# Group normalisation in two batches and weight peaks in three groups, in the front of a recurrent kernel

## The chip, the cores and the metric

The kernel runs on one core of one Trainium2 chip. The metric is the device time of one execution in microseconds (us); the figure for a kernel is the median over its runs. PE is TensorE, PEld its weight loads, DVE VectorE, ACT ScalarE, POOL GpSimd, SP the engine that issues the DMAs.

## The reference, cut to what matters

```python
def _gn(v, G=32, eps=1e-05):                 # v is 8 x 128 x 32 x 32
    g = v.reshape(B_, G, C_ // G, H_, W_)
    m, s = mean and variance of g over (channels of a group, H, W)
    return ((g - m) / sqrt(s + eps)).reshape(v.shape)

def step(h, xr):                             # one row (or column) of 8 images
    gi, gh = xi @ wih.T, h @ whh.T           # 3 gates of 128 channels each
    r, z = sigmoid(ir + hr), sigmoid(iz + hz)
    n = tanh(i_n + r * h_n)
    ctx = (1 - z) * n + z * h
    h_new = tanh(conv1d(ctx, cw, cb))        # 3 taps along the row
    return h_new, ctx

# 32 steps in each of three directions: down, up, and right to left; then
out = x + einsum('bchw,oc->bohw', concat(ctx_d, ctx_u, ctx_r), w_comb) + b_comb
```

## The kernel before

The 128 channels lie on the 128 partitions. Three recurrences (k = 0, 1, 2) of 32 steps run interleaved. Every float32 product is made of three float16 ones: an operand is scaled and split into a high part (`HI`, its float16 rounding) and a low part (`LO`, what is left), and HI·HI, LO·HI and HI·LO are added in PSUM. That holds for weights (`w_parts`), for the normalised images (`x_rows`), for the contexts and for the hidden state.

Each engine has its own instruction stream, written out by hand in the order in which it is to run; an instruction waits on semaphores, and everything behind it in that stream waits with it. SP issues two weight loads (k = 0, 1), eight image loads (512 KB each), then the weights of k = 2 and of the combination.

The front, up to the first real product, does two things.

1. **Weights.** A set of weights (7 of them: the gates and the convolution of each k, and the combination) is scaled by a power of two that comes from its largest row sum. ACT sums magnitudes (`magnitude_sums`, L418), PE turns the sums into rows (`turn_sums`, L811), DVE takes the maximum (`sets_peak`, L642 and L644), PE spreads it over the partitions (`spread_peaks`, L817), DVE makes the scales (`weight_scales`, L653 to L659). Sets 0 to 3 go first, sets 4 to 6 later. Then each of ten units of three weight blocks is split: ACT makes the high part (`weights_hi`, L439), and the low part is made by POOL for four units (`in 0`, `rec 0`, `conv 0`, `in 1`, L388 and L393) and by DVE for six (`weights_lo`, L634).
2. **Images.** DVE takes the mean and variance of six images per channel (`image_stats`, L584 and L589, in the order 0, 2, 3, 5, 6, 7), ACT those of images 1 and 4 (`image_moments`). Then one chain for all eight images: PE averages the means over the groups (L834), DVE makes the deviations (`spread`, L596 to L601), PE averages those (L838), DVE adds epsilon (`variance`, L606), POOL takes the power -1/2 (L398), DVE makes the shift (`shift`, L612). Then both engines normalise the first and last four rows (`edges`, 128x256) of their images (DVE 0 to 4, ACT 5 to 7), and later the last four columns (`strip`, 128x96) and the `core` (128x672). From the normalised rows ACT makes the high part of each piece (`x_hi`, L453) and DVE the low part (`x_lo`, L626).

Between these PE runs products whose result nobody reads (`warm`, L823, 128x512 each): 12 (`FRONT_WARM`) before it waits for the image statistics, 4 (`CHAIN_WARM`) after each of three steps of the chain, and 7 (`LAST_WARM`) after it has waited for the shift (`x_factor`). The first real product (L849, `input_products(0, 0)`) waits for the first `x_hi`.

After that, `opening` (one for each engine) issues the first steps of the three recurrences with the remaining strips, pieces and weight units between them, and `blocks` the steady loop. At the end PE multiplies the contexts with the combination's weights, DVE adds the residual and SP stores.

In the steady part of the code a block needs the split rows, the weights' parts of its direction, and the hidden state of the step before.

Of the kernel before, what the change touches and what calls it, by code (L numbers as in the profile page):

```python
# [99 lines left out]
CORE_ON_ACT = {(1, 1): (5,), (1, 2): (6,), (2, 0): (7,)}  # L100
CORE_ON_DVE = {(1, 1): (0,), (1, 2): (1, 2), (2, 0): (3, 4)}


def build(nc, x_d, w_d, bias_d, out_d):
# [4 lines left out]
    with ExitStack() as ctx:  # L109
# [33 lines left out]
        peak = [sb(f"peak_{n}", [SETS, 1], f32) for n in range(2)]  # L143
        peak_diag = [sb(f"peak_diag_{n}", [SETS, SETS], f32) for n in range(2)]
# [38 lines left out]
        peak_bank = [conv_bank[0], n_bank[2]]  # L183
        avg_bank, var_bank = conv_bank[1], rz_bank[0]
# [176 lines left out]
        def _(pool):  # L361
# [23 lines left out]
            pool.wait_ge(scale_done, 1)  # L385
            for unit in range(len(POOL_UNITS)):
                n, lo, hi = unit_blocks(unit)
                nc.gpsimd.tensor_tensor(out=w_scaled32[:, unit, :], in0=merged(w32[:, lo:hi, :]),  # L388
# [8 lines left out]
            pool.wait_ge(var_eps, 1)  # L397
            nc.gpsimd.tensor_tensor(out=x_scale[:], in0=gvar[:], in1=minus_half[:], op=ALU.pow) \  # L398
                .then_inc(pow_done, 1)

        @block.scalar
        def _(act):
# [33 lines left out]
            def weights_hi(unit):  # L436
                n, lo, hi = unit_blocks(unit)
                act.wait_ge(scale_done, 1 if n < SET_GROUPS[0][1] else 2)
                nc.scalar.activation(w_parts[:, HI, lo:hi, :], w32[:, lo:hi, :], ACT.Copy,  # L439
                                     scale=w_scale[:, n:n + 1]).then_inc(w_hi_done, 1)  # L440

            def normalise(b, cells):

                act.wait_ge(x_factor, 1)
# [83 lines left out]
            def opening():  # L528
# [5 lines left out]
                for b in ACT_NORMED[0:2]:  # L534
                    normalise(b, strip)
# [3 lines left out]
                normalise(ACT_NORMED[2], strip)  # L539
# [29 lines left out]
        def _(dve):  # L569
# [23 lines left out]
            def spread():  # L593

                dve.wait_ge(mean_avg, 1)
                chain(nc.vector.tensor_tensor(out=dev[:], in0=meanvar[:, :, 0], in1=avg_bank[:, 0:B],  # L596
                                              op=ALU.subtract))
                chain(nc.vector.tensor_tensor(out=dev[:], in0=dev[:], in1=dev[:], op=ALU.mult))
                nc.vector.tensor_tensor(out=dev[:], in0=dev[:], in1=meanvar[:, :, 1],
                                        op=ALU.add).then_inc(spread_done, 1)  # L600
                nc.vector.tensor_copy(gmean[:], avg_bank[:, 0:B])  # L601

            def variance():

                dve.wait_ge(var_avg, 1)
                nc.vector.tensor_scalar(gvar[:], var_bank[:, 0:B], EPS, ACT_SCALE ** -2, ALU.add,  # L606
                                        ALU.mult).then_inc(var_eps, 1)

            def shift():

                dve.wait_ge(pow_done, 1)
                nc.vector.scalar_tensor_tensor(x_shift[:], gmean[:], -1.0, x_scale[:],  # L612
# [49 lines left out]
            dve_normed = [b for b in range(B) if b not in ACT_NORMED]  # L662
# [401 lines left out]
```

## Time and profile before

| | |
|---|---|
| time, median of 3 runs | 346.21 us (346.2 to 346.48) |
| the profiled execution | 346.73 us, its span 345.0 us |
| outside the span | 1.73 us |
| PE busy | 321.6 us (93% of the span) |
| DVE, ACT, POOL busy | 294.0, 252.6, 11.0 us |

The span runs from the first to the last instruction that the profiler recorded. Times within a run are given from its start. "Idle before" in a row is the time for which the engine did nothing ahead of that instruction, and the arrow names what ended it. Successive instructions of DVE and ACT overlap by 0.08 to 0.1 us in the records when the second doesn't wait for the first; matmuls overlap by more, so for PE the distance of two starts is what an instruction takes.

### The profile page before, as it was taken

How to read it: one execution, taken by the hardware profiler on the slowest of the kernel's cores; microseconds unless marked ns; L12 is line 12 of the kernel's file. 1: busy time of each engine (PE TensorE's matmuls, PEld its weight loads, DVE VectorE, ACT ScalarE, POOL GpSimd, SP SyncE). 2: the span in 40 equal slices, each digit the busy share in tenths (PEclk: the TensorE clock that was granted, in tenths of full speed). 3: DMA queues.
4: the chain of work that ended last, by engine and by line, in shares of the span. 5: the costliest groups of instructions: out<-in, count | busy, mean ns of one | idle time of the engine just before them, and what ended most of it. 6: DMA issues, size and time to landing. Idle time of an engine off the chain costs nothing.

```text
span 345.0 us, 7730 instructions
## 1 busy us (share of the span) xinstructions
PE 321.6 (93%) x2725; PEld 261.2 (76%) x2725; DVE 294.0 (85%) x781; ACT 252.6 (73%) x587; POOL 11.0 (3%) x24
## 2 busy tenths in 40 slices
PE   0589689999999999999999999999999999999995
PEld 0237568888888888888888888888888888874442
DVE  0878999999999999999989989888888888896342
ACT  5879988888888878788777777777777777767600
POOL 2540000000000000000000000000000000000000
PEclk9999999999999999999999999999999999999999
DMA  7900000000000000000000000000000000000555
GB/s 296 409 10 4 0 2 0 2 1 3 2 0 2 3 0 3 2 0 3 0 0 0 0 0 0 0 0 0 0 0 0 0 0 0 0 2 24 171 151 143
DMA packets 11251, 10.61 MB, mean 31 GB/s; under 512 B 2528, under 2 KB 9824, under 8 KB 11232
## 3 DMA queue, kind: packets, MB, share of 16 engines
q1 hardware_dynamic: 11232, 10.36, 8.9%
q8 instruction: 12, 0.20, 0.2%
q14 instruction: 7, 0.06, 0.1%
HBM read 6.16 MB, written 4.19 MB: 30 GB/s over the span
## 4 chain that ended last, share of the span: by engine, by line
PE 83%; DVE 6%; ACT 6%; DMA 2%; issue 1%; POOL 1%; POOLq 0%; SPq 0%; ACTq 0%; DVEq 0%
PE rz_bank L849 22%; PE conv_bank L849 17%; PE rz_bank L852 11%; PE n_bank L849 11%; PE conv_bank L852 8%; PE n_bank L852 5%; DMA x<-x_dram 2%; PE rz_bank L958 2%; PE n_bank L960 2%; PE n_bank L958 2%; PE rz_bank L960 2%; PE n_bank L962 2%; PE rz_bank L962 2%; ACT w_parts L439 1%; ACT ctx_store L445 1%
## 5 line engine op out<-in xcount | busy, mean ns | idle before, releaser
L849 PE MATMUL conv_bank<-ctx_store,w_parts 128*128 (+1 forms) x558 | 106.9, 273 | 4.7 <-DVE ctx_store L711 2.0
L849 PE MATMUL rz_bank<-x_rows,w_parts 128*128 128x256 f16 (+1 forms) x384 | 78.6, 273 | 0.4 <-ACT x_rows L453 0.4
L849 PE MATMUL rz_bank<-h_parts,w_parts 128*128 128x256 f16 x372 | 76.1, 273 | 0.8 <-DVE w_parts L634 0.8
L488 ACT ACTIVATE nval<-npre 128x256 f32<-128x256 f32 x93 | 38.7, 416 | 52.0 <-DVE npre L718 52.0
L476 ACT ACTIVATE rz<-rz_bank,descale 128x512 f32<-128x512 f32 x96 | 65.9, 686 | 9.2 <-PE rz_bank L849 1.4
L849 PEld LDWEIGHTS conv_bank<-ctx_store,w_parts 128*128 128x128 f16 x558 | 54.0, 97 | 18.6 <-DVE ctx_store L711 3.0
L852 PE MATMUL conv_bank<-ctx_store,w_parts 128*128 (+1 forms) x279 | 66.0, 273 | 0.0
L706 DVE SCALAR_TENSOR_TENSOR npre<-n_bank,descale,rz 128x256 f32<-128x256 f32 x93 | 45.0, 484 | 15.6 <-ACT rz L476 14.4
L852 PE MATMUL rz_bank<-x_rows,w_parts 128*128 128x256 f16 (+1 forms) x192 | 52.2, 273 | 0.0
L493 ACT ACTIVATE hval<-conv_bank,biases,descale 128x256 f32<-128x256 f32 x93 | 51.4, 553 | 0.0
L849 PE MATMUL n_bank<-x_rows,w_parts 128*128 128x256 f16 (+1 forms) x192 | 47.1, 273 | 0.0
L849 PE MATMUL n_bank<-h_parts,w_parts 128*128 128x256 f16 x186 | 45.7, 273 | 0.0
L852 PE MATMUL rz_bank<-h_parts,w_parts 128*128 128x256 f16 x186 | 45.7, 273 | 0.0
L718 DVE SCALAR_TENSOR_TENSOR npre<-n_bank,descale,npre 128x256 f32<-128x256 f32 x93 | 44.4, 477 | 0.0
L499 ACT ACTIVATE ctx_store<-context 128x272 f16<-128x272 f32 (+1 forms) x96 | 40.8, 425 | 2.1 <-DVE context L699 1.4
L699 DVE TENSOR_TENSOR context<-rz,nval 128x256 f32<-128x256 f32 x93 | 39.5, 425 | 3.2
L711 DVE SCALAR_TENSOR_TENSOR ctx_store<-context,ctx_store 128x272 f16<-128x272 f32 (+1 forms) x96 | 41.5, 432 | 0.5 <-ACT ctx_store L499 0.5
L849 PEld LDWEIGHTS rz_bank<-x_rows,w_parts 128*128 128x128 f16 x384 | 37.5, 98 | 5.3 <-issue 0.9
L691 DVE SCALAR_TENSOR_TENSOR nval<-rz,nval 128x256 f32<-128x256 f32 x96 | 40.0, 417 | 0.9 <-ACT nval L488 0.8
L849 PEld LDWEIGHTS rz_bank<-h_parts,w_parts 128*128 128x128 f16 x372 | 36.2, 98 | 5.6 <-DVE w_parts L634 1.1
L729 DVE TENSOR_TENSOR rz<-rz,hval 128x256 f32<-128x256 f32 x93 | 38.8, 417 | 0.0
L723 DVE SCALAR_TENSOR_TENSOR h_parts<-hval,h_parts 128x256 f16<-128x256 f32 x93 | 38.5, 414 | 0.3 <-ACT h_parts L504 0.3
(90 smaller groups left out, 408.9 us busy)
## 6 DMA issues: line engine op xcount, KB each, us to landing
x<-x_dram SPq DMA_DIRECT2D x8, 512.0 KB, 8.8
out_dram<-x_rows SPq DMA_DIRECT2D x7, 512.0 KB, 3.3
ctx_store<-weights_dram SPq DMA_DIRECT2D x3, 576.0 KB, 4.9
out_dram<-x_rows SPq DMA_DIRECT2D x2, 256.0 KB, 2.6
ctx_store<-weights_dram SPq DMA_DIRECT2D x1, 192.0 KB, 12.1
biases<-biases_dram SPq DMA_DIRECT2D x1, 2.0 KB, 11.7
```

The costliest lines, as they stand in the source:

```text
L476: nc.scalar.activation(rz[k][:].rearrange("p g c -> p (g c)"), rz_bank[k][:], ACT.Sigmoid, scale=gate_scale(k)).then_inc(sig_done[k], 1)
L488: nc.scalar.activation(nval[k][:], npre[k][:], ACT.Tanh).then_inc(n_done[k], 1)
L493: nc.scalar.activation(hval[k][:], conv_bank[k % 2][:, 0:COLS], ACT.Tanh, bias=biases[:, k:k + 1], scale=conv_scale(k)).then_inc(h_done[k], 1)
L499: nc.scalar.activation(context_lines(k, s, HI), context[k][:].rearrange("p l b -> p (l b)"), ACT.Copy, scale=ACT_SCALE).then_inc(ctx_hi_do ...
L691: nc.vector.scalar_tensor_tensor(nval[k][:], z, 1.0, nval[k][:], ALU.subtract, ALU.mult).then_inc(zn_done[k], 1)
L699: nc.vector.tensor_tensor(out=context[k][:, 1:1 + LINE, :], in0=lines(zh), in1=lines(nval[k][:]), op=ALU.subtract).then_inc(ctx_done[k], 1)
L706: nc.vector.scalar_tensor_tensor(npre[k][:], n_bank[k][:, COLS:2 * COLS], gate_scale(k), rz[k][:, 0, :], ALU.mult, ALU.mult).then_inc(rh_d ...
L711: nc.vector.scalar_tensor_tensor(context_lines(k, s, LO), context[k][:].rearrange("p l b -> p (l b)"), ACT_SCALE, context_lines(k, s, HI), ...
L718: nc.vector.scalar_tensor_tensor(npre[k][:], n_bank[k][:, 0:COLS], gate_scale(k), npre[k][:], ALU.mult, ALU.add).then_inc(npre_done[k], 1)
L729: nc.vector.tensor_tensor(out=rz[k][:, 0, :], in0=rz[k][:, 1, :], in1=hval[k][:], op=ALU.mult)
L849: last = nc.tensor.matmul(out, w_block(HI, k, n), parts(hi_or_lo), start=start, stop=stop and hi_or_lo == LO, skip_group_check=True)
L852: last = nc.tensor.matmul(out, w_block(LO, k, n), parts(HI), start=False, stop=False, skip_group_check=True)
```

## The change

The images are normalised in two batches, 0 to 3 and 4 to 7: the whole chain (average, `spread`, average, `variance`, power, `shift`) is issued once for each, on four columns instead of eight, into banks of its own. DVE now normalises images 0, 1, 4, 5, 6 and ACT 2, 3, 7. The two images of each engine that belong to the first batch get both edges and strip normalised in the front. The weight sets form three groups, (0, 1), (2, 3) and (4, 5, 6), and the first group's peak and scale stand ahead of all image statistics on DVE, the second's behind image 0. POOL makes the low part of five units (`conv 1` is added) and the low part of `rec 1` moves on DVE from the opening into the front. `FRONT_WARM` goes from 12 to 10, and those products now stand behind PE's second average of the first batch.

```diff
-ACT_NORMED = (5, 6, 7)
-SET_GROUPS = ((0, 4), (4, SETS))
+BATCHES = ((0, 4), (4, B))
+ACT_NORMED = (2, 3, 7)
+DVE_NORMED = (0, 1, 4, 5, 6)
+ACT_STAGES, DVE_STAGES = (0, 5, 6, 9), (0, 7, 10, 15)
+SET_GROUPS = ((0, 2), (2, 4), (4, SETS))
-FRONT_WARM, CHAIN_WARM, LAST_WARM = 12, 4, 7
+FRONT_WARM, CHAIN_WARM, LAST_WARM = 10, 4, 7
-POOL_UNITS = ("in 0", "rec 0", "conv 0", "in 1")
-DVE_UNITS = ("conv 1", "rec 1", "in 2", "conv 2", "rec 2", "comb")
+POOL_UNITS = ("in 0", "rec 0", "conv 0", "in 1", "conv 1")
+DVE_UNITS = ("rec 1", "in 2", "conv 2", "rec 2", "comb")
...
# gpsimd: the power, now after the five units and once for each batch
+            def inverse_deviation(batch):
+                ims = slice(*BATCHES[batch])
+                pool.wait_ge(var_eps, batch + 1)
+                nc.gpsimd.tensor_tensor(out=x_scale[:, ims], in0=gvar[:, ims], in1=minus_half[:, ims],
+                                        op=ALU.pow).then_inc(pow_done, 1)
...
# scalar: the wait of a weight unit, the wait of a piece, and the order
-                act.wait_ge(scale_done, 1 if n < SET_GROUPS[0][1] else 2)
+                act.wait_ge(scale_done, 1 + sum(n >= end for _, end in SET_GROUPS))
...
-                act.wait_ge(x_normed, normed * (B - len(ACT_NORMED)))
-                act.wait_ge(x_normed_act, normed * len(ACT_NORMED))
+                act.wait_ge(x_normed, DVE_STAGES[normed])
+                act.wait_ge(x_normed_act, ACT_STAGES[normed])
...
+            for unit in range(3):
+                weights_hi(unit)
             image_moments(ACT_IMAGES[0])
-            for unit in range(2):
-                weights_hi(unit)
+            weights_hi(UNITS.index("in 1"))
             image_moments(ACT_IMAGES[1])
-            for unit in range(2, UNITS.index("in 2")):
-                weights_hi(unit)
+            for unit in ("conv 1", "rec 1"):
+                weights_hi(UNITS.index(unit))
             for k in (2, COMB):
                 magnitude_sums(k)
-            for b in ACT_NORMED:
-                normalise(b, edges)
+            for cells in (edges, strip):
+                for b in ACT_NORMED[0:2]:
+                    normalise(b, cells)
+            normalise(ACT_NORMED[2], edges)
...
# vector: the order of the front
-            image_stats(0)
             sets_peak(0)
             weight_scales(0)
-            for b in (2, 3, 5, 6, 7):
+            image_stats(0)
+            sets_peak(1)
+            weight_scales(1)
+            for b in (2, 3, 5):
                 image_stats(b)
-            spread()
-            weights_lo(UNITS.index("conv 1"))
-            variance()
-            sets_peak(1)
-            shift()
-            for b in dve_normed:
+            spread(0)
+            image_stats(6)
+            variance(0)
+            image_stats(7)
+            spread(1)
+            shift(0)
+            normalise(DVE_NORMED[0], edges)
+            variance(1)
+            normalise(DVE_NORMED[1], edges)
+            for b in DVE_NORMED[0:2]:
+                normalise(b, strip)
+            weights_lo(UNITS.index("rec 1"))
+            sets_peak(2)
+            shift(1)
+            for b in DVE_NORMED[2:]:
                 normalise(b, edges)
-            normalise(dve_normed[0], strip)
+            normalise(DVE_NORMED[2], strip)
...
# vector: the opening
                 blend(0, 0)
-                for b in dve_normed[1:3]:
-                    normalise(b, strip)
+                normalise(DVE_NORMED[3], strip)
                 context_lo(0, 0)
                 blend(1, 0)
-                for b in dve_normed[3:]:
-                    normalise(b, strip)
+                normalise(DVE_NORMED[4], strip)
                 context_lo(1, 0)
-                weights_lo(UNITS.index("rec 1"))
                 hidden_lo(0, 0)
...
# tensor: the front
-            turn_sums(0)
-            spread_peaks(0)
+            def average(batch, dve_images, act_images):
+                ims = slice(*BATCHES[batch])
+                pe.wait_ge(aggr_done, dve_images)
+                pe.wait_ge(act_stats, 2 * act_images)
+                nc.tensor.matmul(avg_bank[batch][:, ims], group_avg[:], meanvar[:, ims, 0],
+                                 start=True, stop=True).then_inc(mean_avg, 1)
+
+            def average_variance(batch):
+                ims = slice(*BATCHES[batch])
+                pe.wait_ge(spread_done, batch + 1)
+                nc.tensor.matmul(var_bank[batch][:, ims], group_avg[:], dev[:, ims],
+                                 start=True, stop=True).then_inc(var_avg, 1)
+
+            for n in range(2):
+                turn_sums(n)
+                spread_peaks(n)
+            average(0, 3, 1)
             pe.wait_ge(w_hi_done, 2)
+            average_variance(0)
             warm(FRONT_WARM)
-            pe.wait_ge(aggr_done, B - len(ACT_IMAGES))
-            pe.wait_ge(act_stats, 2 * len(ACT_IMAGES))
-            nc.tensor.matmul(avg_bank[:, 0:B], group_avg[:], meanvar[:, :, 0],
-                             start=True, stop=True).then_inc(mean_avg, 1)
+            average(1, B - len(ACT_IMAGES), len(ACT_IMAGES))
             warm(CHAIN_WARM)
-            pe.wait_ge(spread_done, 1)
-            nc.tensor.matmul(var_bank[:, 0:B], group_avg[:], dev[:],
-                             start=True, stop=True).then_inc(var_avg, 1)
+            average_variance(1)
             warm(CHAIN_WARM)
-            turn_sums(1)
+            turn_sums(2)
             warm(CHAIN_WARM)
-            spread_peaks(1)
-            pe.wait_ge(x_factor, 1)
+            spread_peaks(2)
+            pe.wait_ge(x_factor, 2)
             warm(LAST_WARM)
```

The rest of the diff gives `spread`, `variance` and `shift` a batch argument and the columns `ims` of that batch, and moves ACT's strip of its third image a few places up in its opening, with the other two strips gone from there.

## Rows read from the trace of the kernel before

**Rows 1.** Windows: length, busy us and count by engine, clock, DMA share, GB/s.
```profile
24.80:52.00 27.20, 21.73 (x186) 17.18 (x186) 25.11 (x69) 24.19 (x55) 0.00 (x0) 1.00 0.01 2
52.00:306.00 254.00, 253.90 (x2324) 222.97 (x2325) 237.03 (x642) 197.04 (x466) 0.00 (x0) 1.00 0.00 1
```

**Rows 2.** Timeline of DVE, image statistics: start us, length us, what.
```profile
8.19 1.29 DVE L584 BATCH_NORM_STATS2 stats<-x 128x6 f32<-128x512 f32 x2 [8.19 <-DMA x<-x_dram]
...
9.63 0.23 DVE L642 TENSOR_REDUCE peak<-conv_bank 4x1 f32<-4x128 f32 x1
...
11.48 1.28 DVE L584 BATCH_NORM_STATS2 stats<-x 128x6 f32<-128x512 f32 x2
...
16.00 1.23 DVE L584 BATCH_NORM_STATS2 stats<-x 128x6 f32<-128x512 f32 x2
...
17.39 1.23 DVE L584 BATCH_NORM_STATS2 stats<-x 128x6 f32<-128x512 f32 x2
```

**Rows 3.** Timeline of DVE, the chain behind the statistics.
```profile
19.35 0.16 DVE L596 TENSOR_TENSOR dev<-meanvar,conv_bank 128x8 f32<-128x8 f32 x1 [0.48 <-PE conv_bank L834]
...
19.91 0.61 DVE L634 SCALAR_TENSOR_TENSOR w_parts<-ctx_store,w_scale,w_parts 128x384 f16<-128x384 f32 x1
20.43 0.16 DVE L606 TENSOR_SCALAR gvar<-rz_bank 128x8 f32<-128x8 f32 x1
21.59 0.28 DVE L642 TENSOR_REDUCE peak<-n_bank 3x1 f32<-3x128 f32 x1 [0.99 <-PE n_bank L811]
21.90 0.22 DVE L644 TENSOR_SCALAR peak_diag<-unit_diag,peak 3x3 f32<-3x3 f32 x1
...
22.44 1.95 DVE L616 TENSOR_SCALAR ctx_store<-x,gmean,x_scale 128x256 f32<-128x256 f32 x6
```

**Rows 4.** Timeline of PE in the front.
```profile
7.74 0.58 PE L811 MATMUL conv_bank<-unit_diag,abs_sum 128*4 128x128 f32 x2 [7.74 <-ACT x_rows L418]
...
13.49 4.47 PE L823 MATMUL rz_bank<-w_parts 128*128 128x512 f16 x12 [2.74 <-ACT w_parts L439]
18.93 0.39 PE L834 MATMUL conv_bank<-meanvar,group_avg 128*128 128x8 f32 x2 [0.97 <-DVE meanvar L589]
19.17 1.02 PE L823 MATMUL rz_bank<-w_parts 128*128 128x512 f16 x4
...
22.45 0.38 PE L817 MATMUL n_bank<-peak_diag,ones 3*128 3x3 f32 x2
22.76 1.69 PE L823 MATMUL rz_bank<-w_parts 128*128 128x512 f16 x7
24.88 0.27 PE L849 MATMUL rz_bank<-x_rows,w_parts 128*128 128x256 f16 x1 [0.43 <-ACT x_rows L453]
```

**Rows 5.** The chain that ended last: start us, length us, what.
```profile
24.30 0.44 ACT x_rows L453
```

**Rows 6.** Timeline of ACT, weight sums and high parts.
```profile
6.01 0.19 ACT L418 ACTIVATION_READ_ACCUMULATOR x_rows<-ctx_store 128x1 f32 x1
...
12.33 1.10 ACT L439 ACTIVATE w_parts<-ctx_store,w_scale 128x384 f16<-128x384 f32 x2
```

**Rows 7.** Timeline of PE's weight loads during the twelve unread products.
```profile
13.89 0.15 PEld L823 LDWEIGHTS rz_bank<-w_parts 128*128 128x128 f16 x1 [0.28 <-issue]
...
16.88 0.58 PEld L823 LDWEIGHTS rz_bank<-w_parts 128*128 128x128 f16 x3 [0.28 <-issue]
```

**Rows 8.** Groups by form, 18.9 to 26.2 us, a strip: busy us, mean ns.
```profile
L616 DVE TENSOR_SCALAR ctx_store<-x,gmean,x_scale 128x96 f32<-128x96 f32 x1 | 0.3, 331 | 0.0
```

**Rows 9.** Timeline of POOL, the power.
```profile
20.67 1.65 POOL L398 TENSOR_TENSOR x_scale<-gvar,minus_half 128x8 f32<-128x8 f32 x1 [1.03 <-DVE gvar L606]
```

**Rows 10.** Timeline of PE in the opening.
```profile
32.33 0.38 PE L849 MATMUL rz_bank<-h_parts,w_parts 128*128 128x256 f16 x2
...
36.50 0.28 PE L849 MATMUL conv_bank<-ctx_store,w_parts 128*128 128x256 f16 x1 [1.50 <-DVE w_parts L634]
```

**Rows 11.** Timeline of ACT in the opening, the gates of step 1.
```profile
32.91 0.67 ACT L476 ACTIVATE rz<-rz_bank,descale 128x512 f32<-128x512 f32 x1
```

More of the change, by code:

```diff
@@ L142, in build @@
         ones = sb("ones", [SETS, C], f32)
-        peak = [sb(f"peak_{n}", [SETS, 1], f32) for n in range(2)]
-        peak_diag = [sb(f"peak_diag_{n}", [SETS, SETS], f32) for n in range(2)]
+        peak = [sb(f"peak_{n}", [SETS, 1], f32) for n in range(len(SET_GROUPS))]
+        peak_diag = [sb(f"peak_diag_{n}", [SETS, SETS], f32) for n in range(len(SET_GROUPS))]
         image_sum = sb("image_sum", [C, len(ACT_IMAGES)], f32)
@@ L182, in build @@
         y_bank = [rz_bank[0], n_bank[0], rz_bank[1], n_bank[1]]
-        peak_bank = [conv_bank[0], n_bank[2]]
-        avg_bank, var_bank = conv_bank[1], rz_bank[0]
+        peak_bank = [conv_bank[0], n_bank[1], n_bank[2]]
+        avg_bank, var_bank = [conv_bank[1], n_bank[0]], [rz_bank[0], rz_bank[1]]
         w_loaded = [sem(f"w_loaded_{k}") for k in range(DIRS + 1)]
@@ L383, in _ @@
                 nc.gpsimd.memset(context[k][:, 0:PAD:PAD - 1, :], 0.0).then_inc(sides_zero, 1)
-            pool.wait_ge(scale_done, 1)
+            def inverse_deviation(batch):
[3 more added lines that the diff above has]
+                                        op=ALU.pow).then_inc(pow_done, 1)
             for unit in range(len(POOL_UNITS)):
                 n, lo, hi = unit_blocks(unit)
+                pool.wait_ge(scale_done, 1 + sum(n >= end for _, end in SET_GROUPS))
                 nc.gpsimd.tensor_tensor(out=w_scaled32[:, unit, :], in0=merged(w32[:, lo:hi, :]),
@@ L395, in _ @@
                     .then_inc(w_lo_pool, 1)
-            pool.wait_ge(var_eps, 1)
-            nc.gpsimd.tensor_tensor(out=x_scale[:], in0=gvar[:], in1=minus_half[:], op=ALU.pow) \
-                .then_inc(pow_done, 1)
+            for batch in range(len(BATCHES)):
+                inverse_deviation(batch)
         @block.scalar
@@ L442, in normalise @@
             def normalise(b, cells):
-                act.wait_ge(x_factor, 1)
+                act.wait_ge(x_factor, 1 if b < BATCHES[0][1] else 2)
                 nc.scalar.activation(cells(x_norm[:, b // 2, :, :, b % 2]), cells(x32[:, b, :, :]), ACT.Identity,
@@ L533, in opening @@
                 new_value(1, 0)
-                for b in ACT_NORMED[0:2]:
-                    normalise(b, strip)
+                normalise(ACT_NORMED[2], strip)
                 context_hi(1, 0)
@@ L538, in opening @@
                 hidden_hi(0, 0)
-                normalise(ACT_NORMED[2], strip)
                 x_hi(FIRST_COLS[0], 2)
@@ L590, in image_stats, with spread, variance, shift @@
                     .then_inc(aggr_done, 1)
-            def spread():
-                dve.wait_ge(mean_avg, 1)
-                chain(nc.vector.tensor_tensor(out=dev[:], in0=meanvar[:, :, 0], in1=avg_bank[:, 0:B],
+            def spread(batch):
+                ims = slice(*BATCHES[batch])
+                dve.wait_ge(mean_avg, batch + 1)
+                chain(nc.vector.tensor_tensor(out=dev[:, ims], in0=meanvar[:, ims, 0], in1=avg_bank[batch][:, ims],
                                               op=ALU.subtract))
-                chain(nc.vector.tensor_tensor(out=dev[:], in0=dev[:], in1=dev[:], op=ALU.mult))
-                nc.vector.tensor_tensor(out=dev[:], in0=dev[:], in1=meanvar[:, :, 1],
+                chain(nc.vector.tensor_tensor(out=dev[:, ims], in0=dev[:, ims], in1=dev[:, ims], op=ALU.mult))
+                nc.vector.tensor_tensor(out=dev[:, ims], in0=dev[:, ims], in1=meanvar[:, ims, 1],
                                         op=ALU.add).then_inc(spread_done, 1)
[L601 to L606, printed above, removed]
+                nc.vector.tensor_copy(gmean[:, ims], avg_bank[batch][:, ims])
+            def variance(batch):
+                ims = slice(*BATCHES[batch])
+                dve.wait_ge(var_avg, batch + 1)
+                nc.vector.tensor_scalar(gvar[:, ims], var_bank[batch][:, ims], EPS, ACT_SCALE ** -2, ALU.add,
                                         ALU.mult).then_inc(var_eps, 1)
-            def shift():
-                dve.wait_ge(pow_done, 1)
-                nc.vector.scalar_tensor_tensor(x_shift[:], gmean[:], -1.0, x_scale[:],
+            def shift(batch):
+                ims = slice(*BATCHES[batch])
+                dve.wait_ge(pow_done, batch + 1)
+                nc.vector.scalar_tensor_tensor(x_shift[:, ims], gmean[:, ims], -1.0, x_scale[:, ims],
                                                ALU.mult, ALU.mult).then_inc(x_factor, 1)
```

10 lines of the change are left out of this document (5 added, 5 removed).

## The prediction

> **What bounds the kernel now.** I read the windows first. From 52 to 306 us PE is busy for 253.90 of 254.00 us, and nothing that the change touches runs there. So the time is the moment at which PE gets into that stretch, plus a fixed rest. From 24.80 to 52.00 us PE still stands idle for 27.20 - 21.73 = 5.5 us [rows 1]; ahead of that is the front, where PE does no real work at all. The change can move the end in two ways only: by the start of the first real product, now 24.88 us [rows 4], and by the idle time of the opening.
>
> Next I read the chain of waits backwards from that product. It waits for the first x_hi (24.30 us, 0.44 us long) [rows 5], that for the normalised edges, those for the shift, the power, the variance, the averages, and the averages for image 7's statistics on DVE [rows 2, 3]. Once the second image has begun at 11.48, DVE goes from image to image in steps of about 1.4 us (16.00, 17.39) [rows 2]. Behind image 7 it waits: 0.48 us for the mean, 0.99 us before the second peak [rows 3]. Those holes are what two batches could fill.
>
> **The change, step by step on DVE.** The first group's weight sums end at 6.01 + 0.19 = 6.20 [rows 6]. Passing them to PE costs some 0.1, PE's turning product 0.58 [rows 4], and from the reduction to the next image DVE needs 11.48 - 9.63 = 1.85 (peak, PE's spreading, four small operations) [rows 2]. 6.20 + 0.1 + 0.58 + 1.85 = 8.8 (8.77, with a handover of 0.04). Image 0 could start at 8.19, so it starts 0.6 late: the first group is not quite done in the idle time. Image 0 takes 9.63 - 8.19 = 1.44, the second group 1.85 again, images 2, 3 and 5 1.44 each (their data are there: before, all this was over at 16.00). 8.8 + 1.44 + 1.85 + 3 x 1.44 = 16.41, where DVE stood at 16.00.
>
> spread(0) costs 19.91 - 19.35 = 0.56 [rows 3]: 16.97. Image 6 takes 17.39 - 16.00 = 1.39 [rows 2], variance(0) 0.08 (its 0.16 less the overlap), image 7's statistics and their handover to PE 18.93 - 17.39 = 1.54 [rows 2, 4]. So the second average *could* go at 16.97 + 1.39 + 0.08 + 1.54 = 19.98, 1.05 behind the 18.93 of before.
>
> **The step that decides: PE.** PE's stream is now average(0), average_variance(0), ten unread products, average(1). average_variance(0) waits for spread(0), whose third operation ends at 16.98 (0.57 from its first); with 0.06 of handover PE takes it at about 17.05. Before, the twelve products began at 13.49, as soon as two weight units were there [rows 4]. Behind them in PE's stream stands everything else: average(1), for which DVE's spread(1) waits, and behind that on DVE shift(0), every edge and strip; for those wait ACT's normalise and x_hi, and for these PE's real products.
>
> What ten products cost is in the trace. The weight loads of the first products follow each other at (16.88 - 13.89) / 7 = 0.427 us; 512 columns in 0.427 us is the lower level of 1.2 GHz. From about 16.9 on the last three starts fit in 0.7 us, 0.22 each, the 2.4 GHz level [rows 7, 4]. PE had done almost nothing before 13.49, and it will have done as little before 17.05. The float32 average costs 0.24 from start to next start at the high level (18.93 to 19.17) [rows 4], at half the clock 0.48; it would end at about 17.5. If the clock rises after as long a run of products as before (3.4 us), eight of ten run at 0.427 and two at 0.22: 3.86 us, and average(1) goes at 21.36 instead of 19.98. **Held for 1.38 us.** All ten at the low level give 4.27 and 21.77; a rise one and a half microseconds earlier gives about 20.6. The profile's clock column (1.00 throughout) doesn't show these two levels; the durations do.
>
> The Trainium skill, page "TensorE: Matmul & The Clock Gate", Part 1, says that the array starts at the lower clock after idling and that the point at which it rises varies from run to run. The trace agrees in the first part (0.427, then 0.22); the second no row of one execution can show, and it is what the rival of the late clock stands on. The same page, Part 2, says that matmuls stay in program order and only weight loads are pulled ahead: by that the average can't overtake the ten products. The sum above takes the order from the code.
>
> **The rest of the chain.** From the average to the variance it was 20.43 - 18.93 = 1.50 [rows 3, 4]: 21.36 + 1.50 = 22.86. Then DVE: variance 0.08; the edges of image 1, (1.95 - 0.33) / 5 = 0.32 [rows 3, 8]; two strips of 0.33 less 0.09 overlap, 0.48 [rows 8]; rec 1's low part 20.43 - 19.91 = 0.52 [rows 3]; the reduction 0.31 and the diagonal 0.13 [rows 3]. shift(1) at 24.70. The power is 1.65 for eight columns [rows 9]; for four I can say only that it is no more, and no less than nothing. At 1.65 it runs from 23.10 to 24.75 and costs 0.08 at most; below 1.6, nothing. I take nothing: DVE's other work covers it. Were that work gone, it would cost up to 1.65. Three edges follow: 0.09 + 3 x 0.32, ending at 25.84 with the last one's tail. x_hi starts at 25.87, ends at 26.30, and PE could take it at 26.44.
>
> But LAST_WARM comes in the way. The third group's diagonal ends at 24.79, PE spreads it at 24.85, the seven products start 0.31 later (22.76 - 22.45) [rows 4] and take 7 x 0.215 = 1.51: PE is free at 26.67. Before, 22.76 + 1.51 = 24.27 was well ahead of 24.88. First real product at **26.67, 1.79 later** than 24.88.
>
> **Edits costed at nothing.** ACT has its three high parts done 1.6 us after 8.9 (1.10 for two) [rows 6], and both its images by about 16.8, ahead of PE's average(1). The low part of conv 1 on POOL ends near 18.3, ahead of the first power and far ahead of its use. ACT's four operations on images 2 and 3 fit between shift(0) at 22.3 and the end of DVE's shift(1) at 24.87. No DMA is moved.
>
> **The opening.** DVE loses rec 1's low part (0.52) and two strips (0.48), ACT two strips. Little of it was on the path: DVE's removed work stood ahead of operations that waited for ACT anyhow. ACT's gates of step 1 start at 32.91, behind ACT's own queue, while their products were done at 32.33 + 0.38 = 32.71 [rows 10, 11]; with a handover of 0.12 they can go at 32.83. 0.08 us is won, and it carries through to the largest hole, 1.50 us before 36.50 [rows 10], which hangs on DVE's queue behind those gates. Bounds: 0 and, if all of DVE's 1.0 us came off that hole, 1.0. I take 0.08, since the chain from PE to ACT to DVE stays as long.
>
> **Sum.** 1.79 - 0.08 = 1.71 us. On the profiled execution, 346.73 + 1.7 = 348.4 (span 346.7); the median lies 0.52 below that execution: 346.21 + 1.71 = **347.9 us**, 0.5% slower. What a measurement of this kernel can tell from no change is about 0.2%, 0.69 us.
>
> **The rivals.**
> - *No hold on PE.* The clock rises early enough, or the ten products are over by 19.98. Then everything is 1.38 less: 346.21 + 0.33 = 346.54. For it: in the trace the average had 0.97 us to spare [rows 4]. Against: ten products after 17.5 need to take 2.5 us, and at the lower level alone they take 4.27. Chance 0.19.
> - *Faster: the opening's holes shrink.* If the full 1.0 us of freed DVE work comes off the hole before 36.50 and PE is not held, 1.79 - 1.38 - 1.0 = -0.6; with the seven last products not binding either (0.2), -0.8, 345.4. It decides only when PE's hold is below 0.1 us. Against: the waits for ACT in that stretch. Chance 0.13.
> - *Late clock.* If the rise comes only after some 6 us, average(1) goes at 21.77 and the four products behind it take 1.7 instead of 0.9, the next ones too: variance(1) 1.2 to 1.5 later than in the sum, in all 3 to 3.5: 349.5. Chance 0.12.
> - The forecast, PE held by 0.6 to 1.8 us: 347.0 to 348.7, chance 0.56.
>
> **Range.** 346.0 to 349.2 holds the forecast, the rival without hold and the milder half of the late clock; it leaves out 0.12 below and 0.06 above. Slower by over 0.2%: 0.56 + 0.12 = 0.68. Faster: 0.12. Within: 0.20.
>
> **What the new profile would show.** Image 0 on DVE at 8.8; spread(0) at 16.4; the ten unread products on PE from 17.5 to past 21, without a gap before average(1), and DVE idle for 1.4 us or more before spread(1), released by PE; the first real product at 26.7, straight behind the seven. I am wrong if DVE doesn't wait before spread(1), if the first real product starts below 25.6, or if the hole before the convolution of k = 2, step 0 is shorter than 1.2 us.

## The result and the profile after

The changed kernel takes 350.92 us (median of 4 runs, 350.38 to 351.17) against 346.35 for the kernel before: ratio 1.0135, 95% interval 1.0123 to 1.0147. The forecast was 347.9, the range ended at 349.2. The direction was right, the loss is 4.57 us instead of 1.7. The profiled execution is the fastest of the four, 350.38 us (span 348.7).

Timeline of DVE in the changed kernel, front, to be compared with [rows 2, 3].

```profile
8.83 1.28 DVE L593 BATCH_NORM_STATS2 stats<-x 128x6 f32<-128x512 f32 x2
...
10.27 0.22 DVE L654 TENSOR_REDUCE peak<-n_bank 2x1 f32<-2x128 f32 x1
10.53 0.31 DVE L656 TENSOR_SCALAR peak_diag<-unit_diag,peak 2x2 f32<-2x2 f32 x1
11.52 0.16 DVE L665 TENSOR_SCALAR pow<-n_bank 128x2 int32<-128x2 int32 x1 [0.68 <-PE n_bank L836]
11.71 0.91 DVE L668 TENSOR_SCALAR descale<-pow 128x2 f32<-128x2 f32 x1
12.65 0.17 DVE L670 RECIPROCAL w_scale<-pow 128x2 f32<-128x2 f32 x1
12.85 0.55 DVE L671 TENSOR_SCALAR w_scale<-w_scale 128x2 f32<-128x2 f32 x1
13.32 1.27 DVE L593 BATCH_NORM_STATS2 stats<-x 128x6 f32<-128x512 f32 x2
...
17.53 0.10 DVE L606 TENSOR_TENSOR dev<-meanvar,conv_bank 128x4 f32<-128x4 f32 x1
17.68 0.82 DVE L608 TENSOR_TENSOR dev<-dev 128x4 f32<-128x4 f32 x1
...
18.69 1.27 DVE L593 BATCH_NORM_STATS2 stats<-x 128x6 f32<-128x512 f32 x2
...
21.46 0.21 DVE L598 BATCH_NORM_AGGREGATE meanvar<-stats 128x2 f32<-128x12 f32 x1
23.80 0.16 DVE L606 TENSOR_TENSOR dev<-meanvar,n_bank 128x4 f32<-128x4 f32 x1 [2.13 <-PE n_bank L851]
...
25.71 0.61 DVE L646 SCALAR_TENSOR_TENSOR w_parts<-ctx_store,w_scale,w_parts 128x384 f16<-128x384 f32 x1
```

Image 0 starts at 8.83, as worked out. Then four operations on two or four columns, which cost 0.16 to 0.22 us in every other place of this trace, take 0.31, 0.91, 0.55 and 0.82. The second weight group, from its reduction at 10.27 to the next image, costs 13.32 - 10.27 = 3.05 us instead of 1.85, spread(0) 18.69 - 17.53 = 1.16 instead of 0.56. And DVE waits 2.13 us for PE ahead of spread(1).

Timeline of POOL, the same kernel.

```profile
9.91 0.91 POOL L402 TENSOR_TENSOR w_parts<-ctx_store,w_parts 128x384 f16<-128x384 f32 x1
10.78 0.83 POOL L397 TENSOR_TENSOR ctx_store<-ctx_store,w_scale 128x384 f32<-128x384 f32 x1
11.69 0.91 POOL L402 TENSOR_TENSOR w_parts<-ctx_store,w_parts 128x384 f16<-128x384 f32 x1
12.55 0.83 POOL L397 TENSOR_TENSOR ctx_store<-ctx_store,w_scale 128x384 f32<-128x384 f32 x1
...
17.57 0.91 POOL L402 TENSOR_TENSOR w_parts<-ctx_store,w_parts 128x384 f16<-128x384 f32 x1 [0.65 <-ACT w_parts L447]
...
25.07 1.11 POOL L391 TENSOR_TENSOR x_scale<-gvar,minus_half 128x4 f32<-128x4 f32 x1 [3.74 <-DVE gvar L617]
```

The operations that began at 9.91, 11.69, 12.55 and 17.57 end at 10.82, 12.60, 13.38 and 18.48. DVE's four long operations end at 10.84, 12.62, 13.40 and 18.50. Each of them ended when GpSimd's operation was over. Not held were the reciprocal (12.65, 0.17), the statistics, and the operations with their input in PSUM (L654 at 10.27 and L665 at 11.52, both inside an operation of GpSimd).

GpSimd's power held nothing either. The low part of rec 1 (L646), which reads two operands in SBUF, began at 25.71 inside the power of 25.07 to 26.18 and took 0.61 us, as in [rows 3], where GpSimd was idle. In the kernel before, the same kind of operation that is stretched here at 10.53 (`peak_diag`) stands inside the power at 21.90 and takes 0.22 us [rows 3, 9]. So it takes a certain kind of operation on each side.

Timeline of PE, the same kernel, to be compared with [rows 4].

```profile
18.84 0.56 PE L857 MATMUL rz_bank<-dev,group_avg 128*128 128x4 f32 x2 [1.97 <-DVE dev L609]
19.27 4.38 PE L842 MATMUL rz_bank<-w_parts 128*128 128x512 f16 x10
23.48 0.28 PE L851 MATMUL n_bank<-meanvar,group_avg 128*128 128x4 f32 x2
...
27.20 1.69 PE L842 MATMUL rz_bank<-w_parts 128*128 128x512 f16 x7
28.72 0.27 PE L879 MATMUL rz_bank<-x_rows,w_parts 128*128 128x256 f16 x1
```

The ten unread products fill the time from 19.27 to 23.48 without a gap, while image 7's statistics were over at 21.46 + 0.21 = 21.67: the average is held 1.75 us (with 0.06 of handover it could have gone at 21.73). From it to the first real product it is 28.72 - 23.48 = 5.24, forecast 5.31. Later PE is busy throughout, as before (windows, columns as in [rows 1]):

```profile
60.00:310.00 250.00, 250.00 (x2291) 219.69 (x2289) 233.07 (x631) 193.98 (x459) 0.00 (x0) 1.00 0.00 1
```

### The profile page after: what moved, and what is told of

It reads as the page before. It is cut to its first block, busy times and chain, and to the rows that moved or that the text cites. A ratio compares the mean times of both kernels' runs of the same rounds, so it can differ in the third digit from the quotient of the medians.

```text
span 348.7 us, 7759 instructions
## 1 busy us (share of the span) xinstructions
PE 323.1 (93%) x2731; PEld 262.9 (75%) x2731; DVE 296.7 (85%) x792; ACT 252.7 (72%) x587; POOL 13.2 (4%) x27
## 4 chain that ended last, share of the span: by engine, by line
PE 87%; DVE 8%; ACT 2%; DMA 1%; issue 1%; ACTq 0%; DVEq 0%
PE rz_bank L879 22%; PE conv_bank L879 17%; PE rz_bank L882 11%; PE n_bank L879 11%; PE conv_bank L882 8%; PE n_bank L882 5%; PE rz_bank L842 2%; PE rz_bank L988 2%; PE n_bank L992 1%; PE n_bank L990 1%; PE rz_bank L990 1%; PE n_bank L988 1%; PE rz_bank L992 1%; DVE stats L593 1%; DMA ctx_store<-weights_dram 1%
```

## The experiments

The kernel before was run beside each group of experiments; its median there was 346.0 to 346.2. Medians are given with their ratio to it and its 95% interval. The line numbers in rows shift with the edits.

**e1_pool_waits.**

```diff
+            pool.wait_ge(scale_done, 2)
             for unit in range(len(POOL_UNITS)):
```

> GpSimd starts its five units only when the second weight group's scale is made. Theory A (a GpSimd operation with two SBUF inputs keeps DVE's small SBUF operations out until it ends): DVE's second weight group takes 1.85 us again instead of 3.05, image 2 starts at 12.1 instead of 13.3, spread(0) still meets GpSimd and costs up to 0.9 more than 0.56. The ten unread products still hold the second average, everything comes 1.2 us earlier: 349.7. Theory B (those operations are slow by themselves, by their width or by the PE's slow clock): no change, 350.9, DVE's 0.91 us operation is still there.

348.41 us, 1.0067 (1.0050 to 1.0083). Timeline of DVE, then of PE:

```profile
11.69 0.17 DVE L669 TENSOR_SCALAR descale<-pow 128x2 f32<-128x2 f32 x1
...
12.17 1.28 DVE L594 BATCH_NORM_STATS2 stats<-x 128x6 f32<-128x512 f32 x2
...
19.71 0.21 DVE L599 BATCH_NORM_AGGREGATE meanvar<-stats 128x2 f32<-128x12 f32 x1
```

```profile
17.51 4.43 PE L843 MATMUL rz_bank<-w_parts 128*128 128x512 f16 x10
21.73 0.43 PE L852 MATMUL n_bank<-meanvar,group_avg 128*128 128x4 f32 x2
22.01 1.70 PE L843 MATMUL rz_bank<-w_parts 128*128 128x512 f16 x4
```

The operation that took 0.91 takes 0.17, image 2 starts at 12.17: theory A. Its time was missed on the good side (349.7 expected), in part since spread(0) fell between two of GpSimd's operations this time (0.54), which no one had arranged. So 1.8 us was won on DVE, 2.2 in the distance to the kernel before (4.57 and 2.41). The hold stayed (the statistics were over at 19.92, the average went at 21.73). New in this trace: the four products behind the average take 1.54 us to the next one instead of 0.86. In e2 four such products wholly at the lower level take 1.66, so the clock rose during the fourth, near 23.4, 6.3 us after PE took up work at 17.09. This execution, 349.47, had the longest time of the four.

**e2_five_unread.**

```diff
-FRONT_WARM, CHAIN_WARM, LAST_WARM = 10, 4, 7
+FRONT_WARM, CHAIN_WARM, LAST_WARM = 5, 4, 7
```

> FRONT_WARM 5 instead of 10, all else as changed. Theory H (the unread products hold the second average): it goes when image 7's statistics are done, 21.75 us instead of 23.48, DVE waits 0.5 instead of 2.1 us ahead of spread(1), first real product at 27.0 to 27.3, time 349.2 to 349.5. Rival (the clock rises too late for it): the later unread products run at the low level, and half of the 1.7 us or more is given back, 350.1 or above.

350.39 us (349.21 to 350.76), 1.0119 (1.0097 to 1.0142). Timeline of PE:

```profile
21.64 0.59 PE L851 MATMUL n_bank<-meanvar,group_avg 128*128 128x4 f32 x2 [0.16 <-DVE meanvar L598]
22.09 1.87 PE L842 MATMUL rz_bank<-w_parts 128*128 128x512 f16 x4
23.75 0.43 PE L857 MATMUL rz_bank<-dev,group_avg 128*128 128x4 f32 x2
24.04 1.47 PE L842 MATMUL rz_bank<-w_parts 128*128 128x512 f16 x4
```

Of theory H the hold came true, its time did not; the rival's time did. The average goes when its data are there, so the hold was real. But the next products run at the lower level until about 25.0, and nearly all of the 1.8 us is given back (4.39 above before, where it was 4.57). PE stood in the way either by the number of its products or by their speed.

**e3_both.** Both edits together.

> Both edits of the two runs above. If A and H hold and add up: second average at about 20.7 us, first real product near 26.0, time 347.2 to 347.9, still not below before. If only one holds, the time is that of the one.

348.10 us, 1.0064 (1.0047 to 1.0080): 0.2 above the expected span, little better than e1 alone. The second average went at 19.90, earlier than expected, the first real product at 26.43, later. Timeline of DVE:

```profile
20.72 0.50 DVE L609 TENSOR_TENSOR dev<-dev 128x4 f32<-128x4 f32 x1
...
22.21 0.16 DVE L625 SCALAR_TENSOR_TENSOR x_shift<-gmean,x_scale 128x4 f32<-128x4 f32 x1 [0.72 <-POOL x_scale L391]
```

GpSimd's later start put its units beside spread(1) (0.50 instead of 0.16), and the first batch's power behind them: DVE waits 0.72 for it. The cure for one place moved the trouble to another.

**e4_weights_only.** One batch, the rest as changed:

```diff
-BATCHES = ((0, 4), (4, B))
+BATCHES = ((0, B),)
...
-            average(0, 3, 1)
             pe.wait_ge(w_hi_done, 2)
+            pe.wait_ge(aggr_done, 3)
+            warm(FRONT_WARM)
+            average(0, B - len(ACT_IMAGES), len(ACT_IMAGES))
+            warm(CHAIN_WARM)
             average_variance(0)
```

> The weight half of the change alone: three weight groups, the first ahead of the images, five units on GpSimd, rec 1's low part in the front; all eight images in one batch, the ten unread products begin after image 3's statistics. Theory A: DVE's second group takes 3.05 us, image 2 starts at 13.3 (11.48 before), all later steps are 1.7 to 1.8 us late, no hold on PE: 348.0 to 348.2. Theory B gives the same. If neither (the loss belongs to the batches): 346.9.

348.36 us (348.27 to 348.94), 1.0066 (1.0049 to 1.0083), a little above the expected. Timeline of DVE:

```profile
11.77 0.91 DVE L668 TENSOR_SCALAR descale<-pow 128x2 f32<-128x2 f32 x1
```

DVE's operation is 0.91 again and image 2 starts at 13.37. So the weight half alone costs 2.4 us, half of the whole; its unread products begin at 16.43 instead of 13.49, and that is in the 2.4.

**e5_unread_placed.** The changed kernel, PE's front:

```diff
+            pe.wait_ge(w_hi_done, 2)
+            warm(10)
             average(0, 3, 1)
-            pe.wait_ge(w_hi_done, 2)
+            warm(4)
             average_variance(0)
-            warm(FRONT_WARM)
+            warm(6)
             average(1, B - len(ACT_IMAGES), len(ACT_IMAGES))
```

> The changed kernel with its unread products spread over stretches in which PE waits anyway: 10 after the second weight group, 4 between the two averages of the first batch, 6 behind them. Theory C (the loss behind image 7 is the hold plus a clock that rises late, 4 to 6 us after the products begin): the second average goes at 21.75 us, all products behind it run at the higher level, first real product at 27.0, time near 349.0 and less spread over the runs. Rival: the clock falls again in the idle stretches between them, no better than 350.

348.88 us (348.81 to 348.97), 1.0079 (1.0064 to 1.0094). Timeline of PE:

```profile
11.47 4.45 PE L842 MATMUL rz_bank<-w_parts 128*128 128x512 f16 x10
...
21.79 0.39 PE L851 MATMUL n_bank<-meanvar,group_avg 128*128 128x4 f32 x2 [1.27 <-DVE meanvar L598]
...
27.14 0.27 PE L881 MATMUL rz_bank<-x_rows,w_parts 128*128 128x256 f16 x1
```

Twenty unread products instead of ten, and 1.8 us nearer to before (2.80 instead of 4.57): it isn't their number that costs, but where they stand. The average now waits for DVE, and the runs lie within 0.16 us.

**e6_placed_pool.** As e5, with 8 in the first place and

```diff
-                pool.wait_ge(scale_done, 1 + sum(n >= end for _, end in SET_GROUPS))
+                pool.wait_ge(scale_done, 1 if unit == 0 else 2)
```

> As the run before, with 8 products in the first place, and GpSimd makes its first unit at once but starts the other four only when the second weight group's scale is made. If contention (1.2 us in that group, up to 0.6 in spread(0)), hold and clock are the whole loss: image 2 starts at 12.2, second average at 19.9 to 20.4, first real product at 25.2 to 25.6, time 346.4 to 346.9. A remaining loss of over 1 us would show a fourth cause.

347.15 us (347.03 to 347.28), 1.0028 (1.0017 to 1.0039). Timeline of DVE, then of PE:

```profile
12.34 1.28 DVE L593 BATCH_NORM_STATS2 stats<-x 128x6 f32<-128x512 f32 x2
```

```profile
20.13 0.39 PE L851 MATMUL n_bank<-meanvar,group_avg 128*128 128x4 f32 x2 [1.27 <-DVE meanvar L598]
...
25.47 0.27 PE L881 MATMUL rz_bank<-x_rows,w_parts 128*128 128x256 f16 x1
```

Image 2, the second average and the first real product come as expected, but the time is 0.25 above the expected span and 1.07 above before. e10 shows why.

**e7_dummy_tt** and **e8_dummy_memset.** The kernel before, with extra work on GpSimd over DVE's weight group:

```diff
+            pool.wait_ge(x_loaded[0], 16)
+            for n in range(4):
+                nc.gpsimd.tensor_tensor(out=w_scaled32[:, n, :], in0=merged(w32[:, DIRS:DIRS + GATES, :]),
+                                        in1=merged(w32[:, DIRS:DIRS + GATES, :]), op=ALU.mult).then_inc(extra, 1)
+            pool.wait_ge(extra, 4)
```

and for e8 three times `nc.gpsimd.memset(w_scaled32[:], 0.0)` in that place.

> The kernel before, with four extra GpSimd multiplications of two SBUF inputs (128x384, nobody reads them) from 8.2 to about 11.8 us, over DVE's first weight group. Theory A: DVE's small SBUF operations there end when a GpSimd operation ends (one of 0.5 to 0.9 us instead of 0.17), image 2 starts 0.5 to 1.0 us later, 346.5 to 347.1. Theory B: every one of them stays at 0.16 to 0.22 us and the time stays at 346.0.

> The kernel before, with three extra GpSimd memsets (128x1536 float32 each, they read no SBUF) from the arrival of image 0. If it is any use of SBUF by GpSimd that keeps DVE's small SBUF operations out, DVE's peak operation (0.22) or one of the scale operations (0.17) is stretched to the end of a memset, as beside the multiplications (0.76). If it is reading, all stay at 0.16 to 0.22.

e7: 346.33 us, 1.0008 (0.9999 to 1.0017). e8: one run, 347.52 beside 346.11; image 0 landed late in it, at 8.00 instead of 7.42 in e10, so its time isn't the price of the memsets alone. Timeline of DVE in e7, then of DVE and of POOL in e8:

```profile
9.10 0.76 DVE L650 TENSOR_SCALAR peak_diag<-unit_diag,peak 4x4 f32<-4x4 f32 x1
```

```profile
9.71 1.15 DVE L649 TENSOR_SCALAR peak_diag<-unit_diag,peak 4x4 f32<-4x4 f32 x1
...
11.72 0.57 DVE L661 TENSOR_SCALAR descale<-pow 128x4 f32<-128x4 f32 x1
```

```profile
8.02 4.25 POOL L388 MEMSET ctx_store<- 128x1536 f32 x3 [4.62 <-DMA x<-x_dram]
```

In e7 one operation was caught (0.76 instead of 0.22) and image 2 started at 11.22, 0.5 later than in e10. The time came out below the expected span; GpSimd's extra multiplications were over at 10.63, before DVE scaled at 10.73. In e8 the memsets end at 9.44, 10.86 and 12.28 if the 4.25 us are cut in three, and DVE's two held operations at 10.86 and 12.29. A memset reads nothing, so it isn't reading alone that holds these DVE operations. So the kernel before shows theory A too, without any other part of the change.

**e9_batches_only.** The batches alone, on the weight groups of before:

```diff
-SET_GROUPS = ((0, 2), (2, 4), (4, SETS))
+SET_GROUPS = ((0, 4), (4, SETS))
...
-FRONT_WARM, CHAIN_WARM, LAST_WARM = 10, 4, 7
+FRONT_WARM, CHAIN_WARM, LAST_WARM = (4, 2, 6), 4, 6
...
-POOL_UNITS = ("in 0", "rec 0", "conv 0", "in 1", "conv 1")
-DVE_UNITS = ("rec 1", "in 2", "conv 2", "rec 2", "comb")
+POOL_UNITS = ("in 0", "rec 0", "conv 0", "in 1")
+DVE_UNITS = ("conv 1", "rec 1", "in 2", "conv 2", "rec 2", "comb")
...
+            pe.wait_ge(w_hi_done, 2)
+            warm(FRONT_WARM[0])
             average(0, 3, 1)
-            pe.wait_ge(w_hi_done, 2)
+            warm(FRONT_WARM[1])
             average_variance(0)
-            warm(FRONT_WARM)
+            warm(FRONT_WARM[2])
             average(1, B - len(ACT_IMAGES), len(ACT_IMAGES))
```

> The batch half of the change alone, on the weight groups of before: four units on GpSimd, conv 1's and rec 1's low parts in DVE's opening, unread products placed 4, 2 and 6 around the first batch's averages, 6 at the end. If the batches fill DVE's holes as meant: second average at 19.6 us, shift(1) at 22.6, first x_hi at 23.7 (24.30 before), first real product 24.2, time 345.3 to 345.8. Rival (GpSimd's operations stretch spread(0) and the power waits behind GpSimd's units): 346.2 or above.

346.40 us (345.51 to 347.14, 12 runs), 1.0005 (0.9996 to 1.0013). The orders of DVE and ACT go with it: image 0 first again, then the one group of four sets. The traced run (345.76) has its first real product at 24.09, about as expected, and its time in the expected span; spread(0) was held there by 0.26 (0.42 instead of 0.16). The median is no better than before and lies in the rival's span, the best runs are 0.5 below before.

**e10_before_again.** The kernel before, unchanged.

> The kernel before, unchanged, for a second trace. Its first profile (span 345.0) was 0.5 us above the median. Theory D: the images landed late in it; here DVE starts image 0 at about 7.4 us instead of 8.19, the first real product is near 24.3 and the span 344.3. The changed kernel can't use that, since its DVE starts image 0 at 8.8 whenever it lands: then 0.5 us of the measured loss is a gain of before that the first trace hid. Rival: image 0 at 8.2 again, and the 0.5 us came from elsewhere.

345.99 us, span 344.3. Timeline of DVE, then of PE:

```profile
7.42 1.29 DVE L584 BATCH_NORM_STATS2 stats<-x 128x6 f32<-128x512 f32 x2 [7.42 <-DMA x<-x_dram]
...
10.72 1.28 DVE L584 BATCH_NORM_STATS2 stats<-x 128x6 f32<-128x512 f32 x2
...
13.83 1.29 DVE L584 BATCH_NORM_STATS2 stats<-x 128x6 f32<-128x512 f32 x2 [0.20 <-DMA x<-x_dram]
```

```profile
12.76 5.30 PE L823 MATMUL rz_bank<-w_parts 128*128 128x512 f16 x12 [2.77 <-ACT w_parts L439]
18.20 0.39 PE L834 MATMUL conv_bank<-meanvar,group_avg 128*128 128x8 f32 x2
...
24.13 0.27 PE L849 MATMUL rz_bank<-x_rows,w_parts 128*128 128x256 f16 x1 [0.41 <-ACT x_rows L453]
```

Theory D: image 0 landed at 7.42, where it had landed at 8.19 in the execution that the prediction was built on [rows 2]; the traces of e7, e9, e11 and e14 have it before 7.6 as well, those of e12, e13 and e8 at 7.73, 7.82 and 8.00. The first real product is at 24.13, not 24.88. The clock rose later too (twelve products in 5.30 us instead of 4.47), and here it cost nothing: the products were over before the average was to go.

**e11_batches_tuned.** e9 with `warm(2)` instead of `warm(4)` between the second batch's averages, and 5 instead of 6 at the end.

> The batches on the weight groups of before, with 2 instead of 4 unread products between the second batch's averages and 5 instead of 6 at the end. If the scatter of that kernel (345.5 to 347.1) is the clock's rise falling into those four products, the slow runs go: median 345.6, all below 346.2, the first version faster than before (346.1). Rival: the rise then falls into later products and the scatter stays, median 346.4.

346.48 us, 1.0013 (0.9999 to 1.0028). The expectation failed in the median and its rival half came true: six runs at 345.4 to 345.9, six at 347.1 to 347.5. Two such groups of times are called heaps from here on.

**e12_early_f32.** e11 with 3 instead of 2 between the first batch's averages, and

```diff
             spread_peaks(0)
+            for _ in range(5):
+                nc.tensor.matmul(rz_bank[2][:, 0:C], group_avg[:], unit_diag[:],
+                                 start=True, stop=True, skip_group_check=True)
```

> The tuned batches kernel, whose runs fell into two heaps (345.4 to 345.9 and 347.1 to 347.5), with five unread float32 products (128x128) on PE from 10.0 to about 12.7 us and 3 instead of 2 between the first batch's averages. Theory E (the upper heap is a clock that rises late, after the first real products): with PE at work from 10.0 the clock is high before the second batch's averages in every run, one heap remains, median 345.6, below before by 0.4 to 0.5. Rival (the heaps have another cause, such as the landing of the images): both heaps stay.

345.69 us, 0.9998 (0.9982 to 1.0014): eight runs at 345.4 to 345.9, four at 346.5 to 348.0. Four of twelve in the upper heap, where it was six of twelve: that alone shows no difference, and theory E's single heap did not come.

**e13_dense.** e12 with `warm(10)` instead of `warm(6)` ahead of the second average.

> As the kernel with early float32 products (8 of 12 runs at 345.4 to 345.9, four at 346.5 to 348.0), with 10 instead of 6 unread products ahead of the second batch's average, so that PE idles 0.4 instead of 1.3 us there. If the upper runs are a clock that fell in that idle time or rose late, they go: all below 346, median 345.6. Rival (where the clock is still low these ten take 4.3 us and hold the average): some runs at 347 or above, as before.

345.46 us (345.31 to 345.81, 11 runs), 0.9982 (0.9973 to 0.9991): one heap, and faster than before by 0.6 us. None of eleven against four of twelve in e12 could still be chance (by counting, about 1 in 18), against six of twelve in e11 hardly. Timeline of PE:

```profile
16.73 2.32 PE L840 MATMUL rz_bank<-w_parts 128*128 128x512 f16 x10
19.45 0.39 PE L849 MATMUL n_bank<-meanvar,group_avg 128*128 128x4 f32 x2 [0.40 <-DVE meanvar L597]
...
24.03 0.27 PE L880 MATMUL rz_bank<-x_rows,w_parts 128*128 128x256 f16 x1
```

**e14_no_front.** e11 with (0, 0, 0) instead of (4, 2, 6).

> The tuned batches kernel without any unread product ahead of the second batch's average (0, 0, 0 instead of 4, 2, 6). If the upper heap (347.1 to 347.5) is a clock that is low when the real products begin, every run is there or above (347.2 to 348.5), the lower heap is gone, and the profile shows real products of 256 columns 0.213 us apart instead of 0.108. Rival: the time stays at 345.4 to 346, or is between the heaps in all runs.

347.37 us (346.30 to 348.25, 5 runs), 1.0046 (1.0031 to 1.0060): no run lies in the lower heap, as the clock theory says; but two lie below the upper one, where all were expected. Timeline of PE:

```profile
21.34 1.89 PE L840 MATMUL rz_bank<-w_parts 128*128 128x512 f16 x4
23.16 0.42 PE L834 MATMUL n_bank<-peak_diag,ones 3*128 3x3 f32 x2
```

The traced execution was the fastest. The four products from 21.34 all ran at the lower level, the five behind them, from 23.51, at the higher: the clock rose at about 23.2 us, ahead of the real products at 24.60. So real products at the lower level were not seen in any trace.

## Why the prediction was right or wrong

**Right.** The direction; image 0 at 8.8; the ten products as a hold on PE, and who waits behind them; the chain from the second average to the first real product (5.31 forecast, 5.24 measured), with the seven last products as its end; the opening: the hole before the convolution of k = 2 went from 1.50 [rows 10] to 1.34 us, and 0.14 us was won from the first real product to there (11.62 and 11.48 us) where 0.08 was forecast. The power of four columns took 1.02 and 1.11 us and stayed hidden.

**The step that failed** is the cost of DVE's small operations: "the second group 1.85 again" and "spread(0) costs 19.91 - 19.35 = 0.56". Those durations were taken from a place where GpSimd did nothing: before, its units began only behind the single first group, and the chain of the images only when they were nearly over. The change starts GpSimd at 9.0, and puts the second group and spread(0) into the middle of its work. DVE's scalings and the product of spread(0), all within SBUF, then wait until GpSimd's operation of 0.8 to 0.9 us is over, however small they are. That cost 1.20 and 0.60 us; e1 and e6 took the 1.20 away but for 0.1 by starting GpSimd behind the group, wholly or after its first unit. e7 and e8 made the same thing happen in the kernel before. The Trainium skill, page "SBUF — State Buffer", section "SBUF: two separate sides", says that DVE and GpSimd share one pair of ports under an exclusive lock, that whichever starts first has it for the whole instruction while the other fully blocks, and that it concerns DVE operations in a 2-port mode or with two SBUF inputs, the latter only against a GpSimd operation that reads SBUF. The traces agree for GpSimd's multiplications, low parts and memsets: the held operations were scalings and a product within SBUF, those with their input in PSUM were not held, and a memset was enough to hold a scaling (0.57 instead of 0.17). They don't agree for the power, which held neither `peak_diag` nor a low part (0.22 and 0.61, as without it); there the measurement decides. The port and the mode of an operation are in no trace. The prediction didn't weigh this at all, though it had GpSimd at work until 18.3 itself, over both places.

**Mis-sized terms.** The hold: 1.38 forecast, 1.75 measured, since all ten ran at about 0.427 us. From their start to the average it is 4.21 us, and 4.22 in e1, where the clock rose only behind it; the forecast had 3.86. PE had taken up work about 4.6 us before the clock rose, against 3.4 in [rows 7]. e1, e2 and e4 had 6.3, 6.2 and 5.7. The late clock was held to be a rival of 0.12; only four of the traces, those of before, e6, e7 and e14, have the rise within 4 us of PE's first unread product.

Against the forecast of 26.67 for the first real product, 28.72 is 2.05 late: 1.20 for the second group, 0.60 for spread(0), 0.37 for the hold, less 0.12 in the small terms.

**The base.** The first trace of before was an execution in which image 0 landed 0.8 us later than in e10 [rows 2], 0.52 above the median. The prediction noted the 0.52 and carried the difference over unchanged. But before can use an earlier landing and the changed kernel can't: its DVE is busy with the first group until 8.8.

Against e10's trace the sum closes: the first real product went from 24.13 to 28.72, 4.59 us. Image 0 starts 8.83 - 7.42 = 1.41 later; the second group costs 3.05 - 1.85 = 1.20 more than its place in before; 0.29 is saved since before had to wait for the landing of image 5, which the later changed kernel finds there; spread(0) and its variance add 1.16 and about 0.05; the hold 1.75; from the average on, 5.24 instead of the 24.13 - 18.20 = 5.93 of before, a gain of 0.69. 1.41 + 1.20 - 0.29 + 1.21 + 1.75 - 0.69 = 4.59. The last term is what the two batches won. The sum is one of two traced executions, which differ by 4.39 us (350.38 and 345.99); the medians differ by 4.57.

Taking the causes out one after the other: placing the products 1.8 us (e5), keeping GpSimd off the second group and, by its timing, off spread(0) another 1.7 (e6). What is left in e6, 1.07 us, was not taken out by itself, but its trace says where it lies. Its first real product is 1.34 later than e10's: image 0 starts at 8.98, 1.56 later, the second group costs 0.07 more, the landing of image 5 saves 0.28. From image 5 to the average it is 0.59 more, with spread(0) on DVE's path, and from the average on 0.59 less. So between these two traces, without contention and hold, the two batches cost as much ahead of the average as they won behind it, and the first group ahead of the images is the loss. The batches without the regrouped weights, with PE kept at work, give the one version below before by more than its interval (e13).

**Still open.** The two heaps of e11 move with PE's unread work (e13, e14), but none of the profiles fell into an upper heap, so that a low clock under the real products is inferred. A late landing of the images, the rival named ahead of e12, isn't excluded; in e13 it came 0.4 late (7.82) and the run took 345.69. Of the 2.2 us that e1 won, 0.4 is accounted for by no trace. The memsets met only scalings, not a product, and whether a multiplication would hold a low part of DVE's, which the power doesn't, no run shows.

## What to carry to other kernels

A duration read from a trace holds for what ran beside it. When a change moves a small DVE operation within SBUF next to GpSimd's work, or GpSimd's work next to it, look in a trace for that pair; for a scaling or product beside a GpSimd operation like those here, price it at up to the whole of that operation. Operations with a PSUM input weren't held here, but no run moved an operand to PSUM as a cure. Filler work on an engine belongs where that engine waits anyway, never ahead of an operation that others wait for. And before a difference is worked out from one execution, see what set its start: a landing that one kernel can use and the other can't makes the base part of the sum.

## What the runs showed that was not expected

- DVE operations of 0.16 to 0.22 us took up to 0.91 us beside GpSimd's two-input operations of 0.83 to 0.91 and up to 1.15 beside memsets of 1.4, each ending within 0.02 us of GpSimd's; GpSimd's own durations didn't change. Beside GpSimd's power of 1.02 to 1.65 us they kept their time.
- From PE's taking up unread products to the clock's rise from 1.2 to 2.4 GHz it took 2.9 us (e7) to 6.3 us (e1) in executions of near kernels. In e9 and e11, where PE stood still for a while between its products, it took longer still: the first began at 12.81 and 12.90, and the rise came only after 20. Twelve products took 4.47 us in one execution of the same kernel and 5.30 in another.
- GpSimd's power took 1.65 us for eight columns and 1.02 to 1.11 for four.
